# Two pairs of neighbouring layer norms in one transformer kernel, each pair made in one phase

## The reference, cut to what matters

```
def _layernorm(x):                                   # the stack's: no gain, no bias
    mu = mean(x); var = mean((x - mu) ** 2)
    return (x - mu) * rsqrt(var + EPS)               # EPS = 1e-5

x = x + _L0_ffn_ref(_layernorm(x), ...)
    # inside: h = layernorm(y, ln1_w, ln1_b), then a short convolution,
    # causal attention with 16 heads of 8, a projection, y = y + attention,
    # then a mixture of 4 experts on layernorm(y, ln2_w, ln2_b)
...
x = x + _L2_ffn_ref(_layernorm(x), ...)
    # inside: h = w_ln1 * y / sqrt(mean(y * y) + EPS)   (no centring, no bias),
    # then latent attention with 16 heads, y = y + attention, then 8 experts
```

## Time and profile before

| what | value |
|---|---|
| median of 3 runs | 1953.51 us |
| lowest and highest run | 1943.57 and 1965.15 us |
| span of the profiled execution, first to last instruction | 1926.2 us |
| time of the profiled execution beyond its span | not listed; the median run is 27.3 us above the span |
| mean granted clock of TensorE in the profiled execution | 0.849 |
| n0f and n0a, from the barrier to the start of L0f | 233.0 to 265.0 us |
| n2f and n2a, from the barrier to the start of L2f | 1099.6 to 1129.6 us |

### The profile page before, as it was taken

The page is one execution under the profiler, slowest core; times in us unless marked ns, Lnnn a source line. Parts: engine busy times, 40 slices in busy tenths (PEclk is TensorE's granted clock), DMA queues, the critical chain, the costliest instruction groups (busy, mean ns, idle before and its releaser), DMA issues. The chain is left out here.

```text
span 1926.2 us, 24318 instructions
## 1 busy us (share of the span) xinstructions
PE 1542.9 (80%) x9156; PEld 783.5 (41%) x9158; DVE 998.0 (52%) x1384; ACT 708.8 (37%) x1306; POOL 576.9 (30%) x602
## 2 busy tenths in 40 slices
PE   5778738899689996985579857999999857779982
PEld 3355513333334443432244334444454432245541
DVE  3799556778332326763367523333342135568855
ACT  2435224667410003762237532333332222255521
POOL 1478523543111103310024124223311110037650
PEclk7799966899889997996669868999896679979985
DMA  3000010000100001000100010000000000000000
GB/s 94 1 1 1 1 40 1 1 1 2 70 1 0 0 0 46 1 1 8 43 3 1 1 40 1 1 1 1 1 1 1 1 26 0 6 1 2 2 3 22
DMA packets 19153, 20.58 MB, mean 11 GB/s; under 512 B 9803, under 2 KB 15163, under 8 KB 18408
## 3 DMA queue, kind: packets, MB, share of 16 engines
q1 hardware_dynamic: 19048, 19.13, 3.3%
HBM read 17.94 MB, written 1.05 MB: 10 GB/s over the span
## 5 line engine op out<-in xcount | busy, mean ns | idle before, releaser
L1677 DVE TENSOR_REDUCE L2f_nm<-P 128x2 f32<-128x768 f32 (+3 forms) x88 | 99.0, 1126 | 222.4 <-PE P L1582 222.0
L1593 PE MATMUL P<-L2f_qs,L2f_ks 49*128 49x256 f32 (+3 forms) x512 | 148.2, 512 | 17.1 <-DMA L2f_qs<-L2f_mt 17.1
L1652 ACT ACTIVATE L2f_prob<-P 128x512 f32<-128x512 f32 x160 | 89.8, 597 | 188.1 <-PE P L1593 188.1
L997 DVE TENSOR_REDUCE L0f_nm<-P 128x2 f32<-128x768 f32 (+3 forms) x88 | 97.4, 1119 | 53.2 <-PE P L904 53.2
L2160 PE MATMUL P<-L0m_hm,L0m_w 128*128 128x512 f32 x256 | 112.5, 599 | 2.7 <-POOL L0m_hm L2122 2.6
L1509 POOL TENSOR_SCALAR_AFFINE_SELECT L2f_prob<-L2f_prob 128x512 f32<-128x512 f32 x64 | 39.6, 637 | 247.6 <-ACT L2f_prob L1652 247.5
L1593 PEld LDWEIGHTS P<-L2f_qs,L2f_ks 49*128 49x128 f32 x512 | 82.1, 212 | 73.1 <-issue 41.4
L1579 PE MATMUL P<-L2f_ks,L2f_qs 48*128 48x512 f32 (+3 forms) x512 | 107.7, 498 | 0.0
L953 ACT ACTIVATE L0f_prob<-P 128x512 f32<-128x512 f32 x160 | 87.1, 604 | 36.7 <-PE P L915 35.3
L2463 POOL TENSOR_TENSOR L3x_exm<-L3x_exm,L3x_rec 128x2048 f32<-128x2048 f32 x16 | 72.4, 4529 | 26.1 <-DVE L3x_rec L2637 26.1
L2160 PEld LDWEIGHTS P<-L0m_hm,L0m_w 128*128 128x128 f32 x256 | 49.1, 192 | 65.0 <-issue 62.9
(11 more groups left out here) (583 smaller groups left out, 3371.9 us busy)
## 6 DMA issues: line engine op xcount, KB each, us to landing
L0m_w<-in_L0m_w SPq DMA_DIRECT2D x1, 2048.0 KB, 7.9
L0f_va<-in_L0f_va SPq DMA_DIRECT2D x3, 512.0 KB, 4.7
in_xt<-in_x SPq DMA_DIRECT2D x1, 1024.0 KB
L0x_segi<-in_segb SPq DMA_DIRECT2D x1, 1024.0 KB, 5.0
L0m_w<-in_L0m_w SPq DMA_DIRECT2D x1, 1024.0 KB, 9.9
L2f_qs<-L2f_mt SPq DMA_DIRECT2D x64, 2.0 KB, 1.7
out<-out_o SPq DMA_DIRECT2D x4, 256.0 KB, 2.5
L1x_va<-in_va SPq DMA_DIRECT2D x3, 256.0 KB, 3.1
```

Of the source, the lines that this page charges most:

```text
L997: nc.vector.tensor_reduce(S.nm[:, qt, first:first + 2 * many].rearrange("p (i e) -> p e i", e=2), P[:, bank:bank + 2, 0:many * width].rear ...
L1593: m = mm(P[:, bank, at:at + width], S.ks[b % 2][64 * e:64 * e + 49, kt * 128:(kt + 1) * 128], S.qs[b % 2][64 * e:64 * e + 49, pair, q0:q0 ...
L1652: nc.scalar.activation(S.group_prob(b, g)[:, slot, :], P[:, bank, :], ACT.Exp).then_inc(*S.act_done.up())
L1677: nc.vector.tensor_reduce(S.nm[:, qt, first:first + 2 * many].rearrange("p (i e) -> p e i", e=2), P[:, bank:bank + 2, 0:many * width].rear ...
```

## The change

The two calls of `phase_norm` for `n0f` and `n2f` go away. The attention functions now call a new function, `phase_norm_twice`, that reads X and writes both Y and Z. The second buffer for roots is `S.prob[1]`. The second column of the constant `eps` becomes EPS * EPS. A function that no phase calls (`phase_latent`), with its helper `groups_of`, and empty lines at the head of the file are taken out too. The other eight norms are as they were.

```
+def phase_norm_twice(nc, G, name, src, dst, dst2, gain, bias, fetch, sq, sq2):
+    ph = Phase(nc, name)
...
+        @block.sync
+        def _(sp):
+            load_all(sp, ld, [(c[:], v) for c, v in zip(cols, given)])
+            load_all(sp, *fetch)
+
+        @block.tensor
+        def _(pe):
+            for b in range(NB):
+                nc.tensor.matmul(P[:, b, :], G["mean"][:], src[:, b, :], start=True, stop=True).then_inc(*mean_up.up())
+            for b in range(NB):
+                pe.wait_ge(*(squared_by_dve if b % 2 else squared).at(0, b // 2 + 1))
+                nc.tensor.matmul(P[:, 4 + b, :], G["mean"][:], sq[:, b, :], start=True, stop=True).then_inc(*var_up.up())
+
+        @block.vector
+        def _(dve):
+            for b in range(NB):
+                dve.wait_ge(*mean_up.at(0, b + 1))
+                nc.vector.tensor_tensor(dst[:, b, :], src[:, b, :], P[:, b, :], ALU.subtract).then_inc(*cent.up())
+                if b % 2:
+                    dve.wait_ge(*cent.at(0, b + 1))
+                    nc.vector.tensor_tensor(sq[:, b, :], dst[:, b, :], dst[:, b, :], ALU.mult).then_inc(*squared_by_dve.up())
+            dve.wait_ge(*ld.at(0, 16 * len(given)))
+            for b in range(NB):
+                dve.wait_ge(*rstd2.at(0, b + 1))
+                dve.wait_ge(*cent.at(0, b + 1))
+                nc.vector.scalar_tensor_tensor(out=dst2[:, b, :], in0=dst[:, b, :], scalar=gain, in1=sq2[:, b, :],
+                                               op0=ALU.mult, op1=ALU.mult).then_inc(*scaled.up())
+                if bias is not None:
+                    dve.wait_ge(*scaled.at(0, b + 1))
+                    nc.vector.tensor_scalar(dst2[:, b, :], dst2[:, b, :], bias, None, ALU.add).then_inc(*out2.up())
...
+        @block.gpsimd
+        def _(pool):
+            for b in range(0, NB, 2):
+                pool.wait_ge(*cent.at(0, b + 1))
+                nc.gpsimd.tensor_tensor(sq[:, b, :], dst[:, b, :], dst[:, b, :], ALU.mult).then_inc(*squared.up())
+            for b in range(NB):
+                pool.wait_ge(*rstd.at(0, b + 1))
+                pool.wait_ge(*scaled.at(0, b + 1))
+                nc.gpsimd.tensor_tensor(dst[:, b, :], dst[:, b, :], sq[:, b, :], ALU.mult).then_inc(*out.up())
+            pool.wait_ge(*out.at(0, NB))
+
+        @block.scalar
+        def _(act):
+            for b in range(NB):
+                act.wait_ge(*var_up.at(0, b + 1))
+                nc.scalar.activation(sq2[:, b, :], P[:, 4 + b, :], ACT.Ln, bias=G["eps"][:, 1:2], scale=1.0 + EPS).then_inc(*ln2.up())
+                nc.scalar.activation(sq[:, b, :], P[:, 4 + b, :], ACT.Ln, bias=G["eps"][:, 0:1]).then_inc(*ln.up())
+                act.wait_ge(*ln2.at(0, b + 1))
+                nc.scalar.activation(sq2[:, b, :], sq2[:, b, :], ACT.Exp, scale=-0.5).then_inc(*rstd2.up())
+                act.wait_ge(*ln.at(0, b + 1))
+                nc.scalar.activation(sq[:, b, :], sq[:, b, :], ACT.Exp, scale=-0.5).then_inc(*rstd.up())
+    ph.done()
...
-    norm((ld, loads), sq=S.prob[0][:, 0:NB, :])
+    norm((ld, loads), sq=S.prob[0][:, 0:NB, :], sq2=S.prob[1][:, 0:NB, :])
...
-        phase_norm(nc, G, "n0f", X, Y)
-        phase_conv_attention(nc, G, D, lambda fetch, sq: phase_norm(nc, G, "n0a", Y, Z, gain=D["L0_ln1_w"], bias=D["L0_ln1_b"], fetch=fetch, sq=sq))
+        phase_conv_attention(nc, G, D, lambda fetch, sq, sq2: phase_norm_twice(nc, G, "n0a", X, Y, Z, D["L0_ln1_w"], D["L0_ln1_b"], fetch, sq, sq2))
...
-        phase_norm(nc, G, "n2f", X, Y)
-        phase_latent_heads(nc, G, D, lambda fetch, sq: phase_norm(nc, G, "n2a", Y, Z, center=False, gain=D["L2_w_ln1"], fetch=fetch, sq=sq))
+        phase_latent_heads(nc, G, D, lambda fetch, sq, sq2: phase_norm_twice(nc, G, "n2a", X, Y, Z, D["L2_w_ln1"], None, fetch, sq, sq2))
...
-    d["eps"] = np.full((128, 2), EPS, f32)
+    d["eps"] = np.broadcast_to(np.array([EPS, EPS * EPS], f32), (128, 2))
```

More of the change, by code:

```diff
@@ L253, in phase_norm @@
     ph.done()
[L257 to L272, removed]
 def spread_between(main, extra):
@@ L283, in spread_between @@
     return out
+def phase_norm_twice(nc, G, name, src, dst, dst2, gain, bias, fetch, sq, sq2):
+    ph = Phase(nc, name)
+    P = G["P"]
+    step, ld = ph.count("step"), ph.count("ld")
+    given = [v for v in (gain, bias) if v is not None]
+    cols = [ph.sb(f"col{n}", [128, 1]) for n in range(len(given))]
+    gain, bias = ([c[:, 0:1] for c in cols] + [None, None])[:2]
+    mean_up, cent, squared, squared_by_dve, var_up, ln, ln2, rstd, rstd2, scaled, out, out2 = (
+        ph.count(n) for n in ("mean_up", "cent", "squared", "squared_by_dve", "var_up", "ln", "ln2", "rstd", "rstd2", "scaled", "out", "out2"))
+    with nc.Block() as block:
+        @block.sync
[26 more added lines that the diff above has]
+                    nc.vector.tensor_scalar(dst2[:, b, :], dst2[:, b, :], bias, None, ALU.add).then_inc(*out2.up())
+            dve.wait_ge(*scaled.at(0, NB))
+            if bias is not None:
+                dve.wait_ge(*out2.at(0, NB))
+        @block.gpsimd
[19 more added lines that the diff above has]
+    ph.done()
```

325 lines of the change are left out of this document (removed).

## The result

The changed kernel has a median of 1942.62 us over 20 runs (1902.34 to 1963.38), against 1948.49 us over 20 runs of the kernel before (1922.82 to 1972.44). The comparison gives a ratio of 0.989, with a 95% interval of 0.985 to 0.993; the forecast was 0.9966. This ratio sets only the runs within 1.5% of each kernel's fastest against each other, 6 of the 20 runs of the changed kernel and 11 of the 20 of before, and one run of 1902.34 us draws that line for the changed kernel. Much of the 1.1% comes from this choice: the ratio of the two medians is 0.997, which is the forecast. Here that is 1940.0 - 1951.2 = 11.2 us faster, +-9.1.

The account below looks back on a forecast made before the run. It took the serial chains in the barrier-closed norm phases, with ScalarE's table switches, as what counts. Gains of 5.6 + 1.1 = 6.7 us took the median from 1953.5 to 1946.8 us; range 1928 to 1964.

Parts of the forecast that it names:

- The switches: ScalarE in each merged norm phase: eight table loads, seven on the path, 1.31 us per switch, rounds of 5.05 us.
- one-table rival: ScalarE in the merged norms: one table serves Ln and Exp, no load between them; gain of 25.0 us, 1928.5; chance 5%.
- slow switch: ScalarE's switch from Exp back to Ln costs more than the load, up to 4.61 us; 13.1 us slower, 1966.6; chance 12%.
- The ends of the phases: Last products and barrier ahead of L0f and L2f: attention starts 5.6 us and 1.1 us earlier, GpSimd's product about 1.29.
- Loads, removed work: SyncE's fetch stays hidden by the barrier, removed steps lie in the stretch already counted: no further gain or loss.
- the step that took everything outside the phases as unchanged: Outside the merged norm phases: time around the span unchanged; attention phases changing by over 3 us would prove the prediction wrong.
- third rival: L0f and L2f: cold clock lasts longer, 10 us more at low level each, 5 us lost each; 3 us slower; chance 7%.
- the median's distance of 27.3 us from the span: Whole kernel: the median lies 27.3 us above the profiled span, taken as unchanged time around the span.

Follow-up runs that it names:

- the twin: The kernel before without its dead code, every instruction kept; ratio 1.001 against the kernel before, mean 3.3 us less, +-16.1.
- warm runs: Changed kernel plus 18 TensorE multiplications with unused results in each merged phase; ratios 0.989 and 0.995, together 25.8 us faster than before, +-6.0.
- e3: Changed kernel with all eight Ln ahead of all eight Exp in each merged phase; ratio 0.998 against the kernel before, mean 24.0 us less, +-12.3.

## Why the prediction was right in the phases and wrong in the size

- **The switches.** Right. Eight loads in each merged phase, rounds of 5.04 us against 5.05, the switch back at 1.31. The one-table rival and the slow switch both fall: 16 loads stand at the lines of the changed kernel's Ln and Exp, and no gap is longer than the load by more than 0.03 us. The drain of 1380 ns that the Trainium skill gives in "ScalarE: Activation LUTs", section "What ACT_TABLE_LOAD costs", shows in neither direction.
- **The ends of the phases.** Right in sum: 26.48 us (26.4 forecast) and 28.83 (28.9), a gain of 6.7 us (6.7). Inside it GpSimd's product in the first place took 1.50 us beside VectorE's bias step, not 1.29, and the barrier behind it 1.13 as assumed.
- **Loads, removed work.** Right; the fetch is hidden, and no wait took the place of another.
- **What failed** is the step that took everything outside the phases as unchanged, together with the third rival's price. The prediction allowed the attention phases 3 us; they moved by 3.4 (L0f) and 25 us (L2f) in the first profile. Two things stood in its place. The first is scatter: I read one trace, in which L2f's window took 390.3 us, and held it for its length. It is one draw: the same instructions took 410.6 us in the twin. The three runs of before, 21.6 us apart, were the sign; I used that spread for the chances and not to ask which phase spreads. So was the median's distance of 27.3 us from the span, which I took for time around the span: 1.7 us of it is that, the rest is the fast draw. The second is a repeatable effect on the clock, 3.9 us gained in L0f and 1.5 lost in L2f. The third rival had a later rise in both places at 5 us each: it came in L2f, cost 1.5, and in L0f the sign was the other. The warm runs move the total by 17 us, +-8, with the lengths of the norm phases unchanged.
- **The 0.989 itself.** By all 38 runs of the changed kernel in three measurements the gain is 8.7 us +-5.6, which the 6.7 us of the phases and the 2.4 us net in L0f and L2f explain, and the 6.7 alone as well. The medians of the first comparison gave 0.997; the ratio 0.989 rests on which runs it takes, and did not come back in 18 further runs. That the rest was chance in the clock is the likeliest reading, not a thing shown run by run: no profile exists for most of those runs. That the forecast of 0.9966 lay so near the medians is in part luck, with means that scatter by 9 us. Why the clock in L0f and L2f answers to the length and the work of the norm phases stays open.

## What to carry to other kernels

Count the table loads of the order in which activations are issued: two functions in turn pay a load at each change, and a merged loop can turn hidden switches into exposed ones. When two kernels are to be told apart by less than the scatter, find the phase that scatters, take more than one profile, and compare the touched phases barrier to barrier, not the totals. In the phases behind them compare how far one instruction lies from the start of its phase: a difference that comes back in every profile is no scatter. A phase in which TensorE waits for others is a place to try multiplications whose results are not used before the phase behind it is touched.

## What the runs showed of the hardware

- TensorE stood idle for 18.96 us ahead of L2f in the changed kernel and started it at the lower level (0.50 in the first 6.5 us); with 18 multiplications in that time the granted clock was 0.90 over the norm phase, and L2f, whose own first stretch still ran near 0.5 (0.56 and 0.53 in the two windows behind its start), was granted 0.89 over its window, against 0.79 to 0.86 in the five profiles without. What the clock answers to over such a distance these runs do not tell.
- The same 16 multiplications of L0f start 77.3 to 77.7 us into the phase behind two norm phases, 72.4 to 73.8 behind the merged one of 26.5 us, and 77.9 to 78.2 behind those of 21.5 and 37.3 us, in all 17 profiles.
- A product of two tiles on VectorE takes 0.75 us alone and 1.76 when it starts just behind one on GpSimd. GpSimd's takes 1.26 alone, 1.27 beside such a product of VectorE (e3, second place, from 1113.19), and 1.50 with VectorE's bias step beside it, in the changed kernel too. The Trainium skill, "GPSIMD Engine Reference", section "1. Specifications", says that GpSimd's SBUF interfaces are shared with VectorE, with contention when a VectorE instruction has two inputs in SBUF, among other cases. The trace agrees for the product (1.76 against 0.75), which reads two; the bias step reads one tile, and no run here tells which case it is.
- A switch of ScalarE's tables is 1.31 us in both directions with the engine at work, in all fourteen switches inside the changed kernel's merged phases.
